# A batched weighted sum over 12,500 entities: the transfers of W are issued by GpSimd instead of SyncE

## The reference

```python
entities = jnp.einsum('be,le->bl', entity_idxs, W)     # (1024, 12500) x (128, 12500) -> (1024, 128)
s = jnp.sum(entity_idxs, axis=1)
s_safe = jnp.where(s != 0, s, 1.0)
scale = jnp.where(s != 0, 1.0 / s_safe, 1.0)
return entities * scale[:, None]
```

## Time and profile before

| | before |
|---|---|
| time, median of 3 runs | 155.78 us (155.61 to 155.93) |
| span of the profiled execution | 154.0 us |
| left over outside the span, against the median | 1.8 us |
| bytes moved | 58.20 MB, all but 0.07 MB on q1 |
| TensorE matmuls (L414) | 133.2 us busy, 784 of them |
| DVE / ACT busy | 90.6 us / 80.3 us |
| GpSimd busy | 0.5 us |
| share of the 16 DMA engines on q1 | 94.2% of the span |

### The profile page before, as it was taken

One profiled execution on the slowest core, in us unless ns is written; L12 is line 12 of the kernel. 1 busy time (PEld: TensorE's weight loads), 2 busy tenths in 40 slices (PEclk: granted clock), 3 DMA queues, 4 the chain that ended last, 5 costly groups with the idle time before them and its releaser, 6 DMA issues.

```text
span 154.0 us, 2291 instructions
## 1 busy us (share of the span) xinstructions
PE 133.4 (87%) x785; PEld 76.6 (50%) x785; DVE 90.6 (59%) x93; ACT 80.3 (52%) x103; POOL 0.5 (0%) x8
## 2 busy tenths in 40 slices
PE   0198999989989989989989989989989989999900
PEld 0043656545545545546545545545545545545500
DVE  0443975838538528628727826835845746648950
ACT  3462755464474464465456447437527527556720
POOL 1000000000000000000000000000000000000000
PEclk9999999999999999999999999999999999999985
DMA  5999999999999999999999999999999999999220
GB/s 165 320 417 423 412 429 421 412 422 419 421 421 417 422 422 417 426 419 419 421 421 419 421 419 418 424 417 419 426 417 413 432 417 406 349 348 346 90 61 4
DMA packets 13866, 58.20 MB, mean 378 GB/s; under 512 B 1148, under 2 KB 6480, under 8 KB 8228
## 3 DMA queue, kind: packets, MB, share of 16 engines
q1 hardware_dynamic: 13860, 58.13, 94.2%
HBM read 57.60 MB, written 0.52 MB: 377 GB/s over the span
## 4 chain that ended last, share of the span: by engine, by line
DMA 61%; PE 12%; issue 7%; DVE 6%; ACT 5%; SPq 4%; ACTq 0%; DVEq 0%
DMA x_sb<-x_t 61%; PE acc L414 12%; DVE w_parts L308 4%; ACT w_parts L230 3%; ACT act_out L236 1%; SPq L152 1%; SPq L156 1%; DVE w_rest L301 1%; ACT w_parts L224 1%; SPq L170 1%; SPq L190 0%; DVE y_sum L354 0%; SPq L161 0%; SPq L166 0%; DVE low_max L313 0%
## 5 line engine op out<-in xcount | busy, mean ns | idle before, releaser
L414 PE MATMUL acc<-w_parts,x_sb 128*128 128x385 bf16 (+1 forms) x784 | 133.2, 331 | 13.1 <-DVE w_parts L308 7.8
L414 PEld LDWEIGHTS acc<-w_parts,x_sb 128*128 128x128 bf16 (+1 forms) x784 | 76.6, 99 | 69.4 <-issue 16.1
L236 ACT ACTIVATE act_out<-x_sb 128x2048 bf16<-128x2048 uint16 (+4 forms) x31 | 48.0, 1549 | 42.5 <-DMA x_sb<-x_t 42.5
L313 DVE TENSOR_REDUCE low_max<-x_sb 128x2048 uint16 (+4 forms) x31 | 56.5, 1831 | 1.6 <-DMA x_sb<-x_t 1.6
L301 DVE TENSOR_TENSOR w_rest<-w_raw,w_parts 128x1024 f32<-128x1024 f32 (+2 forms) x14 | 15.2, 1091 | 37.8 <-ACT w_parts L224 37.8
L308 DVE TENSOR_TENSOR w_parts<-w_rest,w_parts 128x1024 bf16<-128x1024 f32 (+2 forms) x14 | 15.2, 1093 | 16.0 <-ACT w_parts L230 16.0
L224 ACT ACTIVATE w_parts<-w_raw 128x1024 bf16<-128x1024 bf16 (+2 forms) x14 | 13.3, 955 | 18.4 <-PE acc L414 12.7
L230 ACT ACTIVATE w_parts<-w_rest 128x1024 bf16<-128x1024 bf16 (+2 forms) x14 | 13.1, 943 | 1.9 <-DVE w_rest L301 1.9
L236 ACT ACTIVATION_READ_ACCUMULATOR act_out<-x_sb (+2 forms) x31 | 5.8, 187 | 0.0
L354 DVE TENSOR_TENSOR y_sum<-acc,y_sum 128x128 f32<-128x128 f32 x16 | 4.4, 280 | 0.8 <-ACT y_sum L269 0.7
L269 ACT ACTIVATE y_sum<-acc 128x128 f32<-128x128 f32 x8 | 2.2, 275 | 3.0 <-PE acc L414 2.9
(11 more groups left out here) (7 smaller groups left out, 0.8 us busy)
## 6 DMA issues: line engine op xcount, KB each, us to landing
x_sb<-x_t SPq DMA_DIRECT2D x46, 1024.0 KB, 16.5
w_raw<-w_t SPq DMA_DIRECT2D x12, 512.0 KB, 12.9
x_sb<-x_t SPq DMA_DIRECT2D x3, 512.0 KB, 9.4
x_sb<-x_t SPq DMA_DIRECT2D x4, 256.0 KB, 7.8
out<-y SPq DMA_DIRECT2D x4, 128.0 KB, 2.2
x_sb<-x_t SPq DMA_DIRECT2D x1, 336.0 KB
w_raw<-w_t SPq DMA_DIRECT2D x1, 64.0 KB
w_raw<-w_t SPq DMA_DIRECT2D x1, 42.0 KB
```

The source lines that it names most:

```text
L236: nc.scalar.activation(act_out[0:rows, buf, 0:tiles * n].rearrange("p (j b) -> p j b", j=tiles), low, ACT.Copy, accum_out=low_max[0:rows, ...
L313: nc.vector.tensor_reduce(low_max[0:rows, bass.ds(col, 1)], low, AX.XY, ALU.max).then_inc(dve_checked, count)
L414: return nc.tensor.matmul(acc[:, b, 0:N], x_top[0:rows, s, j, b * P:(b + 1) * P], w_parts[0:rows, s, j, :], start=first, stop=last)
```

## The change

`load_w` moves from SyncE's program into GpSimd's, with the waits on `split_done`. GpSimd issues the 12 transfers of W behind its memsets. SyncE keeps the head's four transfers, all of x, and the output. Its four chunks of block 1 now follow one another without a wait. Ahead of its loop stands one new wait, for ACT's check of the head's second tile, whose place in `x_sb` block 2 overwrites.

```diff
@@ block.gpsimd @@
             nc.gpsimd.memset(low_max[:, :], 0.0).then_inc(ones_set, 1)
 
+            def load_w(m, s):
+                pool.dma_start(w_raw[:, s, :, :].rearrange("p j l -> p (j l)"),
+                               w_blocks[m - 1].rearrange("p j l -> p (j l)")).then_inc(w_in[s], 16)
+
+            load_w(1, 1)
+            pool.wait_ge(split_done, 1)
+            load_w(2, 0)
+            with pool.Fori(1, BLOCKS // 2) as i:
+                for s in range(SLOTS):
+                    m = 2 * i + s
+                    pool.wait_ge(split_done, m)
+                    load_w(m + 1, 1 - s)
@@ block.sync @@
             load_x_head(1)
-            load_w(1, 1)
             load_x(1, 1, 0)
             load_x(1, 1, 1)
-            sp.wait_ge(split_done, 1)
-            load_w(2, 0)
             load_x(1, 1, 2)
             load_x(1, 1, 3)
+            sp.wait_ge(act_checked, CHUNKS)
             with sp.Fori(1, BLOCKS // 2) as i:
                 for s in range(SLOTS):
                     m = 2 * i + s
-                    sp.wait_ge(split_done, m)
-                    load_w(m + 1, 1 - s)
                     for c in range(CHUNKS):
                         free_chunk(m - SLOTS, c)
                         load_x(m, s, c)
```

More of the change, by code:

```diff
@@ L147, in _ @@
             nc.gpsimd.memset(low_max[:, :], 0.0).then_inc(ones_set, 1)
+            def load_w(m, s):
[9 more added lines that the diff above has]
+                    load_w(m + 1, 1 - s)
         @block.sync
         def _(sp):
-            def load_w(m, s):
-                sp.dma_start(w_raw[:, s, :, :].rearrange("p j l -> p (j l)"),
-                             w_blocks[m - 1].rearrange("p j l -> p (j l)")).then_inc(w_in[s], 16)
             def load_x(m, s, c):
```

## The result

| | before | changed |
|---|---|---|
| median of the runs beside each other | 155.86 us (4 runs, 155.61 to 156.00) | 157.59 us (4 runs, 156.89 to 158.04) |
| ratio, 95% interval | | 1.0105 (1.0078 to 1.0133) |
| the same once more, more runs | 155.73 us (30 runs) | 157.05 us (7 runs), 1.0084 (1.0054 to 1.0114) |
| span of the profiled execution | 154.0 us | 155.2 us (an execution of 156.89 us) |

The changed kernel is slower, by 1.3 to 1.7 us. The likeliest case was no change. The median of the first four runs lies 0.2 us above the range, that of the longer series, 157.05 us, inside it.

The account below looks back on a forecast made before the run. The prediction took DMA bytes at 420 GB/s as the bound. Its terms, 0 + 0 + 0 - 0.1 us against a span of 154.0 with 1.8 us around it, gave 155.7 us; range 154.9 to 157.4, no-change case 155.4 to 156.1.

Parts of the forecast that it names:

- likeliest case: Whole kernel: nothing comes of the change; chance 0.40, own range 155.4 to 156.1 us.
- What bounds the kernel: Whole run: bytes at 420 GB/s set the pace; the second of the last loads plus an untouched tail sets the time.
- SyncE's issues and waits: SyncE's program: losing 12 issues and 11 waits gains 0, since a full queue stands ahead of each x chunk.
- The 12 transfers on GpSimd: W's loads on GpSimd's queue: same bytes and engines, so 0, with 0 to +3.0 us kept for the range.
- W overtakes x: Queue order up to the last loads: x chunks land 1.25 us later until the last W; worth 0, 0.37 us cover.
- The start: First microseconds: GpSimd issues W while SyncE issues the head, filling gaps; 0.1 us gain, bounds nothing or 1.4 us.
- The slower rival: All W transfers: one from GpSimd holds the DMA engines longer than one from SyncE; 1.5 us, giving 157.3; chance 0.28.
- The rival of a late TensorE: Block 1's split or block 10's x: late W or TensorE costs 0.5 to 1 us, giving 156.5; chance 0.07.

Follow-up runs that it names:

- w1_late: The changed kernel, but GpSimd waits until all four head transfers have landed before issuing W's first transfer; 1.0161, median 158.38 us.
- x_before_w: The kernel before, all transfers on SyncE, with chunks 0 and 1 of x issued ahead of the wait for the split and of W; 1.0004, 155.89 us.
- w1_pool: The kernel before with only W's first transfer given to GpSimd, the other 11 on SyncE; 1.0070 over nine of twelve runs, median of all twelve 157.26 us.
- w1_pool_x_first: The kernel before with W's first transfer on GpSimd and block 1's chunks 2 and 3 ahead of SyncE's wait for the head's split; 1.0091, 157.31 us.
- w1_ahead_sp: The kernel before, one queue, with SyncE issuing W's first transfer ahead of the head's four; 1.0024, 156.17 us.
- w1_act: The kernel before with only W's first transfer given to ScalarE, ahead of its first wait; 1.0035, 156.40 us.
- w1_mid: The changed kernel, but GpSimd waits for the head's W alone before issuing W's first transfer; 1.0014, 155.90 us.
- w1_sp: The changed kernel with only W's first transfer given back to SyncE behind the head, the other 11 on GpSimd; 1.0013, 156.00 us.

## Why the prediction was wrong, point by point

**What bounds the kernel:** right. Bytes set the pace at 420 GB/s in both, and the end hangs on the landing of the second of the last loads. Its place is 17.1 to 17.6 us ahead of the time of the execution in all but w1_late.

**SyncE's issues and waits, worth 0:** right, shown by x_before_w.

**The 12 transfers on GpSimd, worth 0 with +3.0 as the bound:** right for eleven of them (1.0013, at most 0.5 us), and the middle keeps its 420 GB/s. They land in 8.1 us and not in 2.5 to 3.8. That changed nothing, since it is less than the 15 us at hand. The estimate of 3.1 us for each W, from the 6.15 us for 1 MB that the Trainium skill lists on its page "DMA: Bandwidth & Descriptors", section "Measured (HBM→SBUF, 128 partitions, SWDGE, issued from GpSimd)", doesn't hold here: if each W held the engines for that long, the middle's 420 GB/s would have fallen.

**W overtakes x, worth 0:** right in the middle. TensorE's last 160 matmuls, the second half of block 10 and all behind it, run on from 120.86 with hardly a gap, and its last 48 matmuls wait for their transfer, not for TensorE. TensorE is done with the 112 ahead of them at 120.85 + 18.17 = 139.02, 0.37 us early, which is the forecast's cover. Both are 1.2 us later than forecast (137.82 and 138.19): block 10's third chunk landed at 120.81 instead of 118.27, which is W's 1.25 us and the 1.2 to 1.3 us by which every load is late.

**The start, -0.1 us:** this is the step that failed, in sign and in size. It reads "GpSimd is free at 1.0 us, so it can fill gaps while SyncE issues the head", with "nothing, or all 1.4 us" of gain as its bounds. There was no gain: 302 instead of 304 GB/s from 2 to 7 us, and 387 instead of 416 from 7 to 13. Measured, the term is +1.1 us (w1_pool, where five of the nine runs show nothing) to +1.4 us (w1_pool_x_first). The step bounded the price of the first W beside the head only through TensorE ("by up to 1.25 us ... at the end it costs nothing"). The head's W came 3.4 us late, not 1.25, and TensorE did make that good. What it doesn't cover is the DMA engines themselves: there is no idle share after 10 us in which a lagging engine could catch up. In the first 13 us their mean fell 0.56 us behind that of the kernel before, and the slowest of them 1.75 us behind their mean instead of 0.63. The first chunk of block 1 landed 1.7 us late, and 1.2 us of that were still there at the end. Some 0.14 us of it is the program's later start.

**The slower rival** had the right sign and nearly the right size (157.3 us), but for a reason that fell: 12 x 0.125 us by the price of each. It is 0.4 to 0.5 us for a first W that makes the head late (w1_ahead_sp, w1_act), and about 0.9 us more when GpSimd feeds it at 1.34 us. Its sentence that the slowest engine ends the load is borne out (139.34 us against a mean of 137.62), but so it is in the kernel before (138.15 against 137.07), with no transfer of GpSimd's. That its 157.3 us are near the measured time is luck: a price for each W has no part in it.

**The rival of a late TensorE** named 5 us as the point from which it decides. w1_mid starts block 1 5.7 us late and is level or nearly so. w1_late starts it 8.2 us late and loses 2.5 us, half-clock time and a slower pace included. In the changed kernel block 1 was 2.95 us late (16.06 against 13.11), and TensorE wasn't what ended it.

**What stays open:** why GpSimd's transfer does more harm beside the head than ScalarE's, and whether its later issue has a part in that. The trace gives the 16 updates of a load but doesn't name the engines, so it isn't shown that the same one is slowest all along, nor which. Nor is it shown why the rate dips to 330 GB/s behind a late head at a full share, or why the slowest engine can fall back later on too (in w1_sp's profile from 0.59 us behind the mean in block 1 to 2.07 in block 6). No version measured here beats the kernel before.

## What to carry to other kernels

Where the DMA engines have no idle share, waits of the issuing engine are worth nothing, but so is every hope of catching up: a loss of 0.56 us in the first 13 us is still there at the end, and a load lands with its slowest engine, not with the mean. When a transfer is moved to another queue, ask first what it newly runs beside, and test its first instance apart from the rest. Here one of twelve made the loss, and a wait of 4 us ahead of it took the loss away. Before a busy stretch at the end is read as lag, look what is issued in it.

## What the runs showed of the hardware

- 512 KB from GpSimd's queue beside a full queue of SyncE's landed in 8.1 us, and the sum of both stayed at 420 to 421 GB/s. GpSimd's DMA instruction took 0.53 us of it, 0.66 us for the first, against SyncE's 0.33.
- The head's W landed later when 512 KB from another queue ran beside it. ACT, at 4.98 us in the kernel before, began at 7.23 with ScalarE's (w1_act), at 7.31 with GpSimd's (w1_pool), and at 8.26 and 8.40 with GpSimd's and all of block 1's x behind the head (w1_pool_x_first, the changed kernel).
- The 16 updates of a 1 MB load came 1.2 us apart, first to last, for the first chunk of block 1 in the kernel before and 1.8 us apart for the last one of block 11. In the changed kernel it was 2.9 and 2.8 us. What the engines' mean had lost by the first chunk of block 1, 0.56 us, was 0.55 us at the end.
- TensorE was granted 0.50 of its clock within 9.40 us of idle time (w1_late) and began its next block in that state, at 0.32 us a weight load instead of 0.161.
